# Attention with V projected ahead of the head groups, stored in device memory and loaded back per group

## What is computed

```python
q = rope(norm(x) @ wq)            # 32 heads of 128
k = rope(ctx @ wk)                # 8 key heads of 128
v = ctx @ wv                      # 8 value heads of 128
attn = softmax(q @ k.T / sqrt(128) + mask)
x = x + (attn @ v) @ wo           # 4 query heads share one key and value head
```

## Time and profile before

| | us |
|---|---|
| median of 3 runs | 738.63 |
| lowest, highest run | 735.67, 745.71 |
| the profiled execution | 734.99 |
| its span, first to last instruction | 733.1 |

### The profile page before, as it was taken

The page is one execution under the profiler, slowest core; times in us unless marked ns, Lnnn a source line. Parts: engine busy times, 40 slices in busy tenths (PEclk is TensorE's granted clock), DMA queues, the critical chain, the costliest instruction groups (busy, mean ns, idle before and its releaser), DMA issues.

```text
span 733.1 us, 11917 instructions
## 1 busy us (share of the span) xinstructions
PE 698.3 (95%) x3929; PEld 594.0 (81%) x3929; DVE 551.2 (75%) x1174; ACT 396.2 (54%) x602; POOL 300.6 (41%) x150
## 2 busy tenths in 40 slices
PE   5899999999999999999999999797979999999996
PEld 4678888888888888888888888686969998999985
DVE  5977658648848857765864874757999889998994
ACT  4364535536446446454553644653776666766752
POOL 3342404404503413230440440200268887888780
PEclk9999999999999999999999999999999999999999
DMA  9601021012001202202101200840897788787700
GB/s 321 244 26 72 1 72 57 14 47 80 16 12 59 72 0 72 72 0 72 57 14 56 72 0 0 316 175 4 311 329 305 285 321 317 294 330 303 276 25 15
DMA packets 20292, 93.74 MB, mean 128 GB/s; under 512 B 2609, under 2 KB 3761, under 8 KB 11441
## 3 DMA queue, kind: packets, MB, share of 16 engines
q1 hardware_dynamic: 20272, 93.50, 34.8%
HBM read 93.17 MB, written 0.33 MB: 128 GB/s over the span
## 4 chain that ended last, share of the span: by engine, by line
PE 87%; DVE 5%; DMA 4%; ACT 2%; issue 1%; SPq 0%; POOL 0%; POOLq 0%; DVEq 0%
PE bank L376 21%; PE bank L378 20%; PE bank L377 20%; PE bank L573 10%; PE bank L486 8%; PE bank L650 3%; PE bank L456 2%; DMA ctx_raw<-in_ctx_t 2%; DMA w_hs_sb<-in_w_hs 1%; DMA wqo_raw<-in_wo 1%; ACT probs L769 1%; PE bank L657 1%; PE bank L624 1%; PE bank L423 1%; DVE decay L1238 1%
## 5 line engine op out<-in xcount | busy, mean ns | idle before, releaser
L1395 POOL TENSOR_TENSOR wqo_lo<-wqo_raw,wqo_hi 128x2048 fp32r<-128x2048 f32 x15 | 69.5, 4632 | 207.1 <-ACT wqo_hi L705 175.6
L1070 DVE TENSOR_TENSOR pt_lo<-bank,pt_hi 128x512 fp32r<-128x512 f32 x128 | 87.7, 690 | 62.2 <-ACT pt_hi L779 62.2
L779 ACT ACTIVATE pt_hi<-bank 128x512 fp32r<-128x512 f32 x128 | 75.7, 598 | 66.0 <-PE bank L486 65.7
L1382 POOL TENSOR_TENSOR k_lo<-rope_a,k_hi 128x512 fp32r<-128x512 f32 x32 | 43.4, 1355 | 105.9 <-ACT k_hi L723 105.9
L1031 DVE CUSTOM_DVE_ANT_0 probs<-bank,mask_sb 128x512 f32<-128x512 f32 x128 | 82.2, 686 | 0.1
L486 PEld LDWEIGHTS bank<-ident,probs 128*128 128x128 f32 x512 | 63.6, 141 | 21.5 <-ACT probs L769 3.7
L486 PE MATMUL bank<-ident,probs 128*128 128x128 f32 x512 | 76.1, 274 | 4.6 <-ACT probs L760 3.3
L1425 POOL TENSOR_TENSOR w_out_lo<-w_out_sb,w_out_hi 128x2048 fp32r<-128x2048 f32 x16 | 73.4, 4587 | 17.2 <-ACT w_out_hi L880 17.2
L1430 POOL TENSOR_TENSOR w_gate_lo<-w_gate_sb,w_gate_hi 128x2048 fp32r<-128x2048 f32 x15 | 69.0, 4597 | 19.2 <-ACT w_gate_hi L872 19.2
L769 ACT ACTIVATE probs<-probs,neg_max 128x2048 f32<-128x2048 f32 x31 | 62.0, 2005 | 1.0 <-DVE neg_max L1021 0.6
L573 PE MATMUL bank<-xnT,w_hs_sb 128*128 128x128 f32 x512 | 59.7, 275 | 0.6 <-DMA w_hs_sb<-in_w_hs 0.6
(11 more groups left out here) (186 smaller groups left out, 1709.4 us busy)
## 6 DMA issues: line engine op xcount, KB each, us to landing
w_hs_sb<-in_w_hs SPq DMA_DIRECT2D x16, 1024.0 KB, 4.8
w_gate_sb<-in_w_gate SPq DMA_DIRECT2D x16, 1024.0 KB, 4.8
w_out_sb<-in_w_out SPq DMA_DIRECT2D x16, 1024.0 KB, 6.4
wqo_raw<-in_wq SPq DMA_DIRECT2D x8, 1024.0 KB, 4.8
wqo_raw<-in_wo SPq DMA_DIRECT2D x8, 1024.0 KB, 4.8
decay<-decay_rows SPq DMA_DIRECT2D x16, 512.0 KB, 6.8
ctx_raw<-in_ctx_t SPq DMA_DIRECT2D x3, 1024.0 KB, 11.0
wk_raw<-in_wk SPq DMA_DIRECT2D x8, 256.0 KB, 2.7
```

The lines of the kernel that those rows point to most:

```text
L779: act.activation(pt_hi[t % 3], ring_b[(t + 1) % 2][:, :], ACT.Copy).then_inc(s["pt_hi_ready"], 1)
L1070: dve.tensor_tensor(pt_lo[t % 3], ring_b[(t + 1) % 2][:, :], pt_hi[t % 3].bitcast(F32), ALU.subtract)\
L1395: pool.tensor_tensor(wqo_lo[:, :, :], wqo_raw[:, :, :], wqo_hi[:, :, :].bitcast(F32), ALU.subtract)\
```

## The change

All of V is projected before the loop. 32 tiles (16 tiles of 128 keys, for groups 0 to 3 and then 4 to 7) have the context stationary and 512 weight columns (four groups) moving, so V comes out with its keys on partitions and isn't turned. ACT and DVE split each tile into `pt_hi[tile % 2]` and `pt_lo[tile % 2]` (buffers that the loop uses later), and SP stores both parts in device memory, 256 KB each. Per group SP loads `v_hi` and `v_lo` back, 1024 KB each in rows of 512 bytes. K3 of the next group goes into `attend` at t = 2, its rotation in single steps into DVE's steps 3, 5, 7 and 9; head 0's scores of the next group come between `attend` and `project_out`. The copies, transposes and splits of V leave the loop. `q_low` comes after the rotation of K2. The rotations multiply the sines first, then the cosines in place in PSUM, so their last addition reads PSUM. The high part of wo moves from ACT to POOL; `wq_high` moves behind the first exponential. On SP the load of V for the next group stands ahead of the wait for `project_out` and of the load of wq.

```diff
+ROPE_STEPS = (3, 5, 7, 9)
+def rope_slot(b):
+    return 1 if b == 0 else 0
...
+        v_bank = [bank[5], bank[6]]
+        v_store = [nc.dram_tensor(f"v_{part}", (G // HG, KT, P, HG * DH), F32).ap() for part in ("high", "low")]
...
+            sp.wait_ge(s["ctx_lo_ready"], 4)
+            for h in range(HG):
+                sp.dma_start(wvb_raw[:, :, h * DH:(h + 1) * DH], wv[HG + h]).then_inc(s["wvb_in"], 16)
+            def store_v(tile):
+                half, t = tile // KT, tile % KT
+                sp.wait_ge(s["v_lo_ready"], tile + 1)
+                for store, part in zip(v_store, (pt_hi, pt_lo)):
+                    sp.dma_start(store[half, t, :, :], part[tile % 2].bitcast(F32)).then_inc(v_out[tile % 2], 16)
+            def load_v(half, h):
+                for store, part in zip(v_store, (v_hi, v_lo)):
+                    sp.dma_start(part[:, :, :].bitcast(F32), store[half, :, :, h * DH:(h + 1) * DH].rearrange("t p d -> p t d"))\
+                        .then_inc(s["v_in"], 16)
+            for tile in range(KT):
+                store_v(tile)
...
+            for slot in range(2):
+                sp.wait_ge(v_out[slot], 32 * KT // 2)
+            load_v(0, 0)
+            for tile in range(KT, 2 * KT):
+                store_v(tile)
...
+            for g in range(G - 1):
+                sp.wait_ge(s["qproj_ready"], g + 2)
+                sp.dma_start(wqo_raw[:, :, :], wo[g]).then_inc(s["wo_in"], 16)
...
+                sp.wait_ge(s["pv_ready"], g + 1)
+                load_v((g + 1) // HG, (g + 1) % HG)
+                sp.wait_ge(s["oproj_ready"], g + 1)
+                if g + 2 < G:
+                    sp.dma_start(wqo_raw[:, :, :], wq[g + 2]).then_inc(s["wq_in"], 16)
...
+            def project_v(tile):
+                t = tile % KT
+                if tile < KT:
+                    right_hi, right_lo = wva_hi, wva_lo
+                else:
+                    right_hi, right_lo = wvb_hi, wvb_lo
+                    pe.wait_ge(s["wvb_lo_ready"], 1)
+                if tile >= 2:
+                    pe.wait_ge(s["v_lo_ready"], tile - 1)
                 for c in range(KC):
...
+                    last = pairs(v_bank[tile % 2][:, :], ctx_hi[:, c, keys], ctx_lo[:, c, keys], right_hi[:, c, :],
+                                 right_lo[:, c, :], c == 0, c == KC - 1)
...
                     if t == 2 and not last_head:
-                        project_v_block(g + 1, 1)
+                        project_k_block(g + 1, KB - 1)
+                    if t == 2:
+                        pe.wait_ge(s["v_in"], 32 * (g + 1))
...
+            for b in range(KB):
+                project_k_block(0, b)
+                for t in range(4):
+                    project_v(4 * b + t)
+            for t in range(KT):
...
+                project_v(KT + t)
+            scores(0, range(1))
             with pe.Fori(0, G - 1) as g:
-                scores(g)
-                project_qk_and_first_v(g + 1)
+                scores(g, range(1, HG))
+                project_k_block(g + 1, 0)
+                project_k_block(g + 1, 1)
+                project_q(g + 1)
+                project_k_block(g + 1, 2)
+                transpose_q(g + 1)
                 attend(g, False)
-                transpose_v_block(g + 1, 0)
-                project_v_block(g + 1, 3)
-                transpose_v_block(g + 1, 1)
+                scores(g + 1, range(1))
                 project_out(g)
-                transpose_v_block(g + 1, 2)
...
+            def v_high(tile):
+                act.wait_ge(s["v_mm"], tile + 1)
+                if tile >= 2:
+                    act.wait_ge(v_out[tile % 2], 32 * (tile // 2))
+                act.activation(pt_hi[tile % 2], v_bank[tile % 2][:, :], ACT.Copy).then_inc(s["v_hi_ready"], 1)
...
             with dve.Fori(0, G - 1) as g:
-                mask_scores(g)
-                q_and_k(g + 1)
+                mask_scores(g, range(1, HG))
+                k_rotate(g + 1, 0)
+                k_rotate(g + 1, 1)
+                q_rotate(g + 1)
+                k_rotate(g + 1, 2)
+                q_low(g + 1)
                 pt_low(g, False)
                 scale_out(g)
-                v_low(g + 1, 0)
                 attn_low(g)
-                v_low(g + 1, 1)
+                mask_scores(g + 1, range(1))
                 add_out(g)
-                v_low(g + 1, 2)
```

More of the change, by code:

```diff
@@ L445, in transpose_v_block @@
[L445 to L458, removed]
@@ L460, in scores @@
-            def scores(g):
+            def project_v(tile):
[7 more added lines that the diff above has]
+                    pe.wait_ge(s["v_lo_ready"], tile - 1)
+                for c in range(KC):
+                    if tile == 0:
+                        pe.wait_ge(s["wva_lo_ready"], c // 2 + 1)
+                    keys = slice(t * P, (t + 1) * P)
+                    last = pairs(v_bank[tile % 2][:, :], ctx_hi[:, c, keys], ctx_lo[:, c, keys], right_hi[:, c, :],
+                                 right_lo[:, c, :], c == 0, c == KC - 1)
+                last.then_inc(s["v_mm"], 1)
@@ L462, in scores @@
+            def scores(g, heads):
                 pe.wait_ge(s["qT_lo_ready"], g + 1)
-                for h in range(HG):
+                for h in heads:
                     for b in range(KB):
@@ L764, in exps @@
                 for h in range(HG):
+                    if h == 1 and not last_head:
+                        wq_high(g + 1)
                     act.wait_ge(s["neg_max_ready"], HG * g + h + 1)
@@ L797, in _ @@
             ctx_high(0, PAIRS[1])
-            act.wait_ge(s["wq_in"], 16)
-            for two, done in zip(PAIRS, (s["first_wq_hi"], s["wq_hi_ready"])):
-                act.activation(wqo_hi[:, two, :], wqo_raw[:, two, :], ACT.Copy).then_inc(done, 1)
+            act.wait_ge(s["wva_in"], 64)
+            for two in PAIRS:
+                act.activation(wva_hi[:, two, :], wva_raw[:, two, :], ACT.Copy).then_inc(s["wva_hi_ready"], 1)
             act.wait_ge(ctx_in[1], 16)
@@ L1022, in row_max, with mask_scores @@
                     .then_inc(s["neg_max_ready"], 1)
-            def mask_scores(g):
-                for h in range(HG):
+            def mask_scores(g, heads):
+                for h in heads:
                     for b in range(KB):
@@ L1075, in pt_low @@
                         inverse_sums_low(g)
+                    if not last_head and t in ROPE_STEPS:
+                        k_rotate_step(g + 1, KB - 1, ROPE_STEPS.index(t))
             def scale_out(g):
@@ L1115, in _ @@
             ctx_low(0, 2, PAIRS[1])
[L1116 to L1119 removed]
+            for i, two in enumerate(PAIRS):
+                dve.wait_ge(s["wva_hi_ready"], i + 1)
+                dve.tensor_tensor(wva_lo[:, two, :], wva_raw[:, two, :], wva_hi[:, two, :].bitcast(F32), ALU.subtract)\
+                    .then_inc(s["wva_lo_ready"], 1)
@@ L1120, in _ @@
             ctx_low(1, 3, PAIRS[0])
+            v_low(0)
             ctx_low(1, 4, PAIRS[1])
+            v_low(1)
             first_k_rotate(0)
+            v_low(2)
+            ctx_low(2, 5)
+            v_low(3)
+            v_low(4)
+            first_k_rotate(1)
+            v_low(5)
+            ctx_low(3, 6)
+            for tile in range(6, 9):
+                v_low(tile)
+            first_k_rotate(2)
+            for tile in range(9, 13):
+                v_low(tile)
+            first_k_rotate(3)
@@ L1141, in _ @@
                 add_out(g)
[L1142 to L1143 removed]
+            mask_scores(G - 1, range(1, HG))
             pt_low(G - 1, True)
@@ L1376, in split_weight, with k_low @@
                     .then_inc(lo_done, 1)
-            def k_low(g):
-                for b in range(KB):
+            def k_low(g, blocks):
+                for b in blocks:
                     blk = slice(b * 512, (b + 1) * 512)
                     pool.wait_ge(s["k_hi_ready"], KB * g + b + 1)
-                    pool.tensor_tensor(k_lo[:, blk], rope_a[:, (b + 1) % 2, :], k_hi[:, blk].bitcast(F32),
+                    pool.tensor_tensor(k_lo[:, blk], rope_a[:, rope_slot(b), :], k_hi[:, blk].bitcast(F32),
                                        ALU.subtract)\
```

309 lines of the change are left out of this document (132 added, 177 removed).

## The result

The changed kernel takes 770.32 us, the median of 4 runs (769.37 to 774.03); the kernel before took 740.17 beside it (4 runs). The ratio is 1.0437, 95% interval 1.0387 to 1.0486. The range of 732 to 776 holds it, but 752 us falls short: in the profiled executions the span went from 733.1 to 767.6, +34.5 us, where the sum had +14.5.

What follows compares the result with a forecast made beforehand. PE's own instructions were taken to bound the loop (PE busy 95% of the span). Terms -14.1 + 20.3 + 2.8 + 6.5 - 1.0 = +14.5 us gave 749.5 or 753.1, forecast 752 us, range 732 to 776.

Steps and rivals of the forecast that it cites:

- V transposes: Loop, PE: removing 32 fours of V transposes at 0.44 us each saves 14.1 us.
- Wait at tile 1: Tile 1 of `attend`: PE waits 2.9 us for the late `q_low` in each of seven passes, +20.3 us.
- Rival C: Tile 1 of `attend`: `q_low` isn't late, so the 20.3 us fall away; 732 us, 725 with faster start; chance 0.2.
- Rope steps in `attend`: DVE in `attend`: four added rotation steps of 0.70 us cost 0.4 us a pass, 2.8 us in all.
- A loop pass of 50 us: Profile sign of being right: a loop pass takes 50 us, from 59.5 - 10.9 of V - 1.8 + 3.3.
- Loads in the loop: Loop DMA: wq lands behind 2 MB of V yet just in time, so cost 0, with no slack.
- Rival B: Loop DMA: V's rows 256 KB apart load slowly, wq is 2.5 us late per pass; 770 us, chance 0.2.
- The start: Before the loop: waits behind stores and loads sum to 11.1 us against 3.5 + 1.1 saved, +6.5 us (0 to 20).
- at 370 GB/s 28.6 us ... that store lands at about 32: Start: 10.6 MB ahead of the first store; it lands at about 32 us, so V4 idles PE 5.2 us.
- Stores pace the start (D): Start: landings above 3.6 us pace the V tiles; at 4.5 us, 12 us more, 764 us; chance 0.15.
- Last group: Last group: ACT no longer has wo's high part ahead of its exponentials, -1 us of the 3.3 us wait.

Runs made afterwards that it cites:

- e2: Changed kernel with K3's projection moved ahead of tile 1's wait for `q_low` instead of behind it at tile 2; 750.35 us, ratio 1.0165.
- e4: Changed kernel with the first load of V, and its wait for stores, behind all 32 stores instead of the first 16; 763.79 us, ratio 1.0339.
- e5: Changed kernel with K3 ahead of the wait, first V load behind all stores, and input loads issued between stores in order of need; 735.4 us, ratio 0.9972.
- e9: e5 with DVE doing `q_low` and tile 0's split before K2's rotation, K2's `k_hi` behind tile 2, K3's steps at 5, 7, 9, 11; 735.62 us, 0.9955.
- e3: Changed kernel with the stores of tiles 0 and 1 issued ahead of the four loads of wv's second half; 770.72 us, ratio 1.0454.
- e8: Kernel before, with `q_low` behind K2's and K3's rotations and two idle DVE multiplications in front of it; 754.72 us, ratio 1.0209.
- e7: e2 with four idle DVE multiplications ahead of `q_low`; 798.3 us, ratio 1.0831.
- e10: Kernel before, with `q_low` behind K2's and K3's rotations and three idle DVE multiplications in front of it; 772.9 us, ratio 1.0419.
- e11: Kernel before, with `q_low` behind K2's and K3's rotations and four idle DVE multiplications in front of it; 815.06 us, ratio 1.1015.
- e12: e2 with three idle DVE multiplications ahead of `q_low`; 779.0 us, ratio 1.0525.

## Why the prediction was right or wrong

- **V transposes, -14.1.** Right as far as the sum can tell: no such instruction is left, and the sum below closes with this term.
- **Wait at tile 1, 2.9 x 7 = +20.3.** Right in place, cause and count; 2.67 x 7 = 18.7. e2 took it away. Rival C (the wait isn't there) is out.
- **Rope steps in `attend`, +0.4 a pass.** The first pass is 49.86: 46.8 of PE's work (59.5 - 10.9 - 1.8) and 2.67 of wait leave 0.4.
- **"A loop pass of 50 us".** Wrong from the second pass on, and this is one failed step: the sum priced a pause of PE at its length and nothing for what PE's clock does behind it. Six passes had 3.4 us of low clock and 1.37 us more: +8.2. In the loop before PE never paused, but outside it the same trace had two waits of this length: behind the 3.3 us ahead of the last group's `attend` the granted clock is 0.70 from 474.27 to 480.00, a stretch of 3.4 us at half, and behind the 3.5 us at the first Q rotation it is 1.00. So the price could have been bounded, from 0 to half of 3.4 us a pass, 0 to 12 us in seven.
- **Loads in the loop, 0.** Right: V landed 9.4 us after its first issue (forecast 9.4), wq landed 12.2 us after `attend`'s end (12.3), the four exponentials ended 6.3 us after K0's start (6.5). Rival B is out: the Trainium skill, "DMA: Bandwidth & Descriptors", section "Latency and other measured facts", has 207 GB/s for copies between tensors in device memory with rows 512 KiB apart; here 2.1 MB of rows 256 KB apart came in 9.4 us, latency and two issues included, which is 223 GB/s and was early enough for wq.
- **The start, +6.5.** Wrong by 13.7: tile 0 of group 0 starts 89.4 us later than before, where 69.2 is work moved there (324 V matmuls of 0.2275, less K3's 2.73 and four transposes of 0.44), so +20.2. The step that failed is "at 370 GB/s 28.6 us ... that store lands at about 32". The window from 0 to 30.6 us ran at 321 GB/s, so that 10.6 MB need 33 us; and two stores, not one, had to land, the first with an issue of 2.43 us. 38.5 instead of 32, and V4 waited 9.32, not 5.2. Tile 20 waited 5.20 (4 forecast, within its bounds). Of the rest, some 6 us, about 4 are clock again: in these two windows it is 0.64 and 0.76, and 3.0 and 5.1 us of half clock lie behind the two waits. The bound of 20 was just passed.
- **Stores pace the start (D).** Out: in the median a store lands in 2.1 to 2.3 us, under the 2.7 to 3.3 I had taken.
- **Last group, -1.0.** 2.0 instead of 3.3: -1.3.

Sum: -14.1 + 18.7 + 2.8 + 8.2 + 20.2 - 1.3 = 34.5, the change of the span. The start's 20.2, the 0.4 a pass and the 1.37 a pass are what the other terms leave, so that the sum closes proves the split only in part; e2, e4 and e5 test its pieces. The measured medians differ by 30.2, since the profiled execution of before lies 5.2 us under its median and that of the changed kernel 0.95.

Why the mended kernel (e5) isn't 14 us faster: a pass of 48.0 is 1.2 above 46.8, 8.4 us in seven, of which 0.7 a pass is the wait at tile 2 and the rest goes with DVE's extra steps in `attend`, which no run tested by themselves; the start keeps 2.9, and the last group saves 1.3. That leaves -4. By their ratios e5 and e9 lie 2 and 3 us under the kernel before, with intervals that hold 4.

## What to carry to other kernels

Where one engine is the bound, look for what covers each of its waits before taking work off it: the V blocks that the change removed were the cover of `q_low`, and moving one independent block ahead of the wait brought back 20 of 30 us. Price a pause of TensorE above its length: here pauses of 2.7 us and more in a stream of matmuls cost up to 3 us extra, since half clock mostly came with them. Moving a wait can also shift which pauses are hit, as in e3 and e4, so read the passes and not the total alone. Before stores are put behind loads on one queue, add up the bytes ahead at the rate that this stretch really had, and count all the stores that must land.

## What was not expected of the hardware

**Half clock behind short pauses.** Pauses at tile 1 in passes of 48 to 71 us of nearly unbroken matmuls: at 0.97, 1.4 and 1.86 us none of the seven passes of a run had low clock; at 2.67 six of seven after the change and seven of seven in e3 and in e4, at 3.05 four of seven, at 3.53 six of seven had, mostly 3.4 us of it at a price of 0.7 to 1.6 us; at 5.3 and 8.4 us all had 6.8 us or more. What decides within 2.67 to 3.53 stays open, and no pass was run between 1.86 and 2.67. Outside the loop length tells even less: in the last group of the ten runs of the changed kernel PE stands 2.0 us and, 1 us later, another 1.1; nine had low clock there and e9 had none. At the first Q rotation a wait of 2.8 us had low clock in e8, and 3.5 us in the kernel before had none.

**A multiplication of DVE with both inputs in SBUF got longer beside POOL's subtractions; the same size with an input in PSUM didn't.** (SBUF is the on-chip memory that the loads land in, PSUM the one that TensorE's products land in.) DVE's timeline of the kernel before with four added multiplications, and POOL's:

```profile
212.07 7.99 DVE L1012 TENSOR_TENSOR xnT<-cos_k,sin_k 128x512 f32<-128x512 f32 x4
220.09 0.69 DVE L1001 TENSOR_TENSOR qT_lo<-bank,qT_hi 128x512 fp32r<-128x512 f32 x1
```

```profile
212.90 1.71 POOL L1385 TENSOR_TENSOR k_lo<-rope_a,k_hi 128x512 fp32r<-128x512 f32 x1 [1.44 <-ACT k_hi L723]
214.57 4.94 POOL L1398 TENSOR_TENSOR wqo_lo<-wqo_raw,wqo_hi 128x2048 fp32r<-128x2048 f32 x1
```

The first two took the usual 0.69. The third began at 213.52, inside POOL's 1.71 us, and the fourth at 215.19, inside its 4.94; they took 1.64 and 4.87 us and each ended 0.55 us after POOL's instruction had. In the run with two multiplications both took 0.69, for POOL's instructions started after them; in that run the split of a tile of probabilities, with one input in PSUM, took 0.69 at 199.93 inside POOL's 4.60 us from 198.92 on. The Trainium skill, "SBUF — State Buffer", section "SBUF: two separate sides", says that a VectorE operation with two SBUF inputs and a GpSimd operation that reads SBUF take one port pair in turns, whichever starts first for its whole length; the trace agrees. It is why the pauses of e7, e10, e11 and e12 came out longer than meant, and what the change's in-place step in PSUM spares the Q rotation: its last addition takes 0.69 us after the change, at 209.46 inside POOL's `k_lo` of 208.78 to 210.08, and took 1.22 before, at 180.49 inside POOL's `k_lo` of 179.87 to 181.16.

**An issue can hold SP for long.** Four loads of 256 KB took 9.44 us to issue, and the store behind them 2.43, where most stores after it took 0.32 to 0.51. Moved behind two stores they still took 9.11; in e5, issued two by two between later stores, 0.55 to 0.89 each. What holds the issue was not tested by itself.
